# Eight attention heads on five engines: count products set among the scores, the last bias added early, a send moved by six blocks

## What is computed

```python
def gat_layer(x, W, a_src, a_dst, bias, src, dst, heads, out_c, concat):
    h = (x @ W).reshape(n, heads, out_c)
    al_s = jnp.einsum('nhc,hc->nh', h, a_src)
    al_d = jnp.einsum('nhc,hc->nh', h, a_dst)
    e = jax.nn.leaky_relu(al_s[src] + al_d[dst], NEG_SLOPE)
    m = jax.ops.segment_max(e, dst, num_segments=n)
    ex = jnp.exp(e - m[dst])
    z = jax.ops.segment_sum(ex, dst, num_segments=n)
    out = jax.ops.segment_sum(h[src] * (ex / (z[dst] + 1e-16))[:, :, None], dst, num_segments=n)
    out = out.reshape(n, heads * out_c) if concat else out.mean(axis=1)
    return out + bias
# block 3
h = gat_layer(x, W1, a_src1, a_dst1, b1, src, dst, heads=8, out_c=96, concat=True)
h = jax.nn.elu(h)
out = gat_layer(h, W2, a_src2, a_dst2, b2, src, dst, heads=1, out_c=768, concat=False)
x = _layernorm(x + out)
```

## Time and profile before

| | |
|---|---|
| median of three runs | 1436.75 us (1436.01 to 1437.41) |
| profiled execution, its own time | 1437.73 us |
| its span, first to last instruction | 1436.0 us, mean granted clock 0.991 |
| TensorE busy | 1367.7 us (95%) |
| VectorE, ScalarE, GpSimd busy | 762.8, 441.9, 559.0 us |
| chain of work that ended last | PE 76%, DVE 13%, ACT 4%, issue 3%, POOL 3%, DMA 1% |
| the one-head layer of block 2, its score steps | about 1115 to 1143 us |
| the eight heads | about 1266 to 1352 us |
| the last layer | about 1352 to 1436 us |

### The profile page before, as it was taken

The page is one execution under the profiler, slowest core; times in us unless marked ns, Lnnn a source line. Parts: engine busy times, 40 slices in busy tenths (PEclk is TensorE's granted clock), DMA queues, the critical chain, the costliest instruction groups (busy, mean ns, idle before and its releaser), DMA issues.

```text
span 1436.0 us, 22503 instructions
## 1 busy us (share of the span) xinstructions
PE 1367.7 (95%) x7784; PEld 1274.6 (89%) x7784; DVE 762.8 (53%) x1818; ACT 441.9 (31%) x936; POOL 559.0 (39%) x629
## 2 busy tenths in 40 slices
PE   5999999999999999999999999999998999988997
PEld 3676999999999999999999999999888887878874
DVE  6876755224544356474232434765375504599644
ACT  1564521102010000100110222255574424467631
POOL 8000324324243525343442423143433463548830
PEclk9999999999999999999999999999999999998999
DMA  3101111113333223242211211221101310200001
GB/s 117 55 29 34 39 34 50 50 34 109 105 107 105 67 89 115 72 131 68 67 55 45 68 53 46 61 83 57 56 23 39 107 53 17 82 18 1 1 11 54
DMA packets 57804, 86.49 MB, mean 60 GB/s; under 512 B 6468, under 2 KB 54459, under 8 KB 57584
## 3 DMA queue, kind: packets, MB, share of 16 engines
q1 hardware_dynamic: 45204, 65.82, 15.8%
q10 hardware_dynamic: 12504, 19.36, 4.4%
HBM read 83.24 MB, written 1.92 MB: 59 GB/s over the span
## 4 chain that ended last, share of the span: by engine, by line
PE 76%; DVE 13%; ACT 4%; issue 3%; POOL 3%; DMA 1%; DVEq 0%; SPq 0%; ACTq 0%; POOLq 0%
PE psum L2487 13%; PE psum L2491 13%; PE psum L2490 13%; PE psum L2504 7%; PE psum L2507 7%; PE psum L2988 4%; DVE max_scratch L2189 3%; PE psum L2636 3%; PE psum L2561 2%; POOL w_lo L919 2%; PE psum L2530 1%; PE psum L2533 1%; PE psum L2476 1%; DVE more_tiles L2233 1%; DVE score_tiles L2233 1%
## 5 line engine op out<-in xcount | busy, mean ns | idle before, releaser
L2487 PE MATMUL psum<-w_lo,xT_hi 128*125 128x384 f32 (+4 forms) x1110 | 377.4, 340 | 3.3 <-POOL w_lo L919 1.8
L2491 PE MATMUL psum<-w_hi,xT_hi 128*125 128x384 f32 (+4 forms) x1110 | 373.4, 336 | 0.0
L2490 PE MATMUL psum<-w_hi,xT_lo 128*125 128x384 f32 (+4 forms) x1110 | 373.3, 336 | 0.0
L906 POOL CAST w_hi<-w_raw 128x384 fp32r<-128x384 f32 x190 | 105.2, 553 | 569.7 <-PE psum L2491 466.0
L1093 ACT ACTIVATE h_hi<-psum 125x384 fp32r<-125x384 f32 (+1 forms) x120 | 59.1, 492 | 529.3 <-PE psum L2491 524.9
L1739 DVE TENSOR_TENSOR h_lo<-psum,h_hi 125x384 fp32r<-125x384 f32 (+1 forms) x120 | 66.9, 558 | 288.0 <-ACT h_hi L1093 287.2
L2487 PEld LDWEIGHTS psum<-w_lo,xT_hi 128*125 128x125 f32 (+1 forms) x1110 | 205.9, 186 | 6.1 <-POOL w_lo L919 3.4
L908 POOL TENSOR_TENSOR w_lo<-w_raw,w_hi 128x384 fp32r<-128x384 f32 x190 | 201.2, 1059 | 15.2
L2490 PEld LDWEIGHTS psum<-w_hi,xT_lo 128*125 128x125 f32 (+1 forms) x1110 | 206.4, 186 | 0.4
L2491 PEld LDWEIGHTS psum<-w_hi,xT_hi 128*125 128x125 f32 (+1 forms) x1110 | 206.0, 186 | 0.0
L2504 PE MATMUL psum<-h_lo,adjacency 125*125 125x384 f32 (+3 forms) x600 | 203.5, 339 | 2.1 <-issue 1.9
(11 more groups left out here) (350 smaller groups left out, 2272.2 us busy)
## 6 DMA issues: line engine op xcount, KB each, us to landing
w_raw<-weights_dram SPq DMA_DIRECT2D x296, 192.0 KB, 2.4
score_w_raw<-weights_dram ACTq DMA_DIRECT2D x58, 192.0 KB, 2.8
x_nat<-x_dram SPq DMA_DIRECT2D x1, 1875.0 KB
x_residual<-x_dram SPq DMA_DIRECT2D x5, 375.0 KB
score_a_rows<-L_gnn_a_src_dram ACTq DMA_DIRECT2D x8, 192.0 KB, 3.3
score_a_rows<-L_gnn_a_dst_dram ACTq DMA_DIRECT2D x8, 192.0 KB, 4.5
out_dram<-x_residual SPq DMA_DIRECT2D x4, 375.0 KB
rgcn_bias<-rgcn_bias_dram SPq DMA_DIRECT2D x1, 1125.0 KB
```

The source lines that it names most:

```text
L906: nc.gpsimd.tensor_copy(mem.wh[:, slot, :], mem.raw[:, raw_slot, :]).then_inc(w_hi_ready, 1)
L2487: ins = nc.tensor.matmul(o, h, wl, start=(j == 0), stop=False, skip_group_check=True)
L2490: nc.tensor.matmul(o, l, wh, start=False, stop=False, skip_group_check=True)
L2491: ins = nc.tensor.matmul(o, h, wh, start=False, stop=stop and j == k - 1, skip_group_check=True)
```

## The change

Four edits:

1. `Q1` sends its columns at block 22 instead of 16 (`LONG_EVENTS`); `Q3` keeps 16.
2. VectorE's two `finish` of a head move from the next round into the head's own scores, behind score 2, and `columns` moves from before score 4 to before score 2.
3. ScalarE takes the exponent of tile 2 before the below-zero step of tile 3, and GpSimd's round becomes: product of tile 2 of h+1, `unit_sum(h-1)`, products of tiles 3 and 4, `unit_bias(h)`.
4. The bias of `Q3` is loaded into `par[0]` ahead of `Q2`'s features, with a semaphore of its own, and GpSimd's five adds stand ahead of the first head's products.

```diff
+LONG_EVENTS = {3: (("scores", 0),), 6: (("row", 0),), 22: (("send", 0),)}
...
-Q1 = Attention(Q0, 1, D, K8, PIECES, True, BASE_L2B, True, PAIR_EVENTS, {})
+Q1 = Attention(Q0, 1, D, K8, PIECES, True, BASE_L2B, True, LONG_EVENTS, {})
...
-        LATE = 3
+        LATE, COLUMNS_AT, FINISH_AT = 3, 2, 2
...
+            pool.wait_ge(last_bias_loaded, 16)
+            pool.wait_ge(xT_lo_ready, T_Q[2] + UNITS)
+            for m in range(NB):
+                r = mem.xres[0:BP, m, :]
+                nc.gpsimd.tensor_tensor(r, r, mem.par[0][0:BP, 0:D], ALU.add).then_inc(res_biased, 1)
+
+            def late_products(h, a, e):
 
-            def late_products(h):
-
-                for i, counts in enumerate(late_counts):
+                for i, counts in list(enumerate(late_counts))[a:e]:
...
-            late_products(0)
+            late_products(0, 0, LATE)
             for h in range(LAST):
-                late_products(h + 1)
-                unit_bias(h)
+                late_products(h + 1, 0, 1)
                 if h:
                     unit_sum(h - 1)
+                late_products(h + 1, 1, LATE)
+                unit_bias(h)
             unit_sum(LAST - 1)
             split_to(NCHUNKS)
-
-            pool.wait_ge(params_loaded, 16 * 9)
-            pool.wait_ge(cols_ready, Q3.head0 + 1)
-            for m in range(NB):
-                r = mem.xres[0:BP, m, :]
-                nc.gpsimd.tensor_tensor(r, r, mem.par[1][0:BP, 0:D], ALU.add).then_inc(res_biased, 1)
...
             load_row("L3_gnn_b1", par[1], D)
+            load_part("L3_gnn_b2", par[0], 0, D, last_bias_loaded)
...
                 source_below(h, NB - LATE)
-                for k in range(NB - LATE, NB):
+                source_exp_below(h, NB - LATE)
+                source_below(h, NB - LATE + 1)
+                for k in range(NB - LATE + 1, NB):
                     if k + 1 < NB:
                         source_below(h, k + 1)
                     source_exp_below(h, k)
...
-            load_row("L3_gnn_b2", par[1], D)
...
                 for k in range(NB):
-                    if k == NB - 1 and h + 2 < HEADS3:
+                    if k == COLUMNS_AT and h + 2 < HEADS3:
                         columns(Q2, h + 2)
                     score(Q2, h, k)
+                    if k == FINISH_AT:
+                        for i in range(NB - LATE):
+                            finish(Q2, h, i)
...
                 if h:
                     head_z(h - 1)
-                for k in range(NB - LATE):
-                    finish(Q2, h, k)
                 if h + 3 < HEADS3:
                     maxima(Q2, h + 3)
```

More of the change, by code:

```diff
@@ L565, in program @@
         b2_loaded = sem("b2_loaded")
+        last_bias_loaded = sem("last_bias_loaded")
         pre_loaded = [sem(f"pre_loaded{i}") for i in range(PRE_RING)]
```

## The result

The changed kernel takes 1456.4 us (1456.07 to 1458.61, four runs), the kernel before 1436.67 beside it: 1.014 times as long, interval 1.0123 to 1.0158. That is 19.7 us slower; forecast were 14.5, 1451.2, with a range to 1456.0. The profiled execution has a span of 1454.9 for 1436.0, 18.9 more.

What follows compares the result with a forecast made beforehand. TensorE is busy nearly throughout; in the heads VectorE sets turns 1 to 4, ScalarE 5 and 6. Heads +16.8, send +1.4, last layer -3.7 give +14.5 on the median 1436.75: 1451.2 us, range 1439 to 1456.

Steps and rivals of the forecast that it cites:

- The bound before: Eight heads, kernel before: VectorE sets turns 1 to 4 at 11.4 us, ScalarE turns 5 and 6 at 9.4.
- Turn 0: First score of head 0 to that of head 1: +3.6 us, columns waiting for two bias adds; lower bound +1.5.
- Turns 1 and 2: Heads 1 and 2, GpSimd not yet behind: turns of 10.4 and 11.0 us, free of its contention.
- Turn 6: Head 6, no columns left: 10.4 + 2.0 = 12.4 us against 9.4, +3.0.
- Turns 3 to 5: Heads 3 to 5, GpSimd behind: 11.0 plus 1.8 us contention (bounds 0 and 2.9), turns of 12.8.
- The end: Head 7's first score to the end of TensorE's sum: 17.2 us for 11.87, +5.3, waiting for GpSimd's products.
- The send: One-head layer: TensorE stops 1.58 us earlier but resumes 1.4 later, +1.4; bounds -1.6 and +1.4.
- The last layer: Without GpSimd's five adds: -1.9 us from freed count products, -1.8 from TensorE's higher clock; -3.7, bounds -1.9 and -3.7.
- the clock term: Last layer's first sum: with its wait down to 1.5 us, TensorE runs at 2.4 GHz, -1.8.
- Rival (a): Heads: GpSimd's wait doesn't collide, columns and products run alone; +2.9 us, 1439.7; chance 0.12.
- Rival (b): Heads: VectorE alone sets turns 1 to 4 at 10.4, last two turns stay 9.4; faster, 1427.5 us; chance 0.09.
- Rival (c): Heads: columns wait three times, TensorE falls to 1.2 GHz in longer gaps before its sums; +20 or so, 1457; chance 0.07.

Runs made afterwards that it cites:

- the products back in the next round: The changed kernel with VectorE's two count products of a head moved back from among its scores into the next round: 1448.83 us, 1.0087 times the kernel before.
- the pair free: The kernel before with GpSimd's first product of a head waiting for VectorE's two count products of that head: 1436.81 us, 0.9995 times.
- without the heads' orders: The kernel before with only the last bias loaded ahead of the heads and GpSimd's five adds ahead of the first head's products: 1436.61 us, 0.9993 times.
- the heads alone: The kernel before with only the new orders of VectorE, ScalarE and GpSimd in the eight heads; send and bias as before: 1455.45 us, 1.0126 times.
- the last round put back: The changed kernel, but in the last round GpSimd makes all three products of head 7 before unit_sum of head 5: 1452.7 us, 1.011 times.
- the send alone: The kernel before with only the one-head layer's send moved to block 22 from 16: 1439.44 us, 1.0014 times.
- GpSimd's order back: The changed kernel with GpSimd's round as before (three products, bias add, unit_sum last): 1443.93 us, 1.0046 times the kernel before.
- ScalarE's order back: The changed kernel with ScalarE's below-zero steps of tiles 2 and 3 again before the exponent of tile 2: 1459.15 us, a single execution.

## Why the prediction was right and wrong, point by point

Direction, mechanism and place were right: slower, through the heads, by GpSimd's wait for the elu and ScalarE's loop closing over VectorE's fourth score. The time lies 0.4 beyond the upper end of the range, since two terms of the sum were taken too low: the price of contention in turns 3 to 5, and the clock at the end of the heads. The range itself was drawn narrow: with the prediction's own upper bound for the heads, +22, the sum is 1456.5.

- **The bound before** (VectorE in turns 1 to 4, ScalarE in 5 and 6): right. With the products back in the next round turn 6 is 9.5, and with the pair free turns 1 and 2 are 10.3, for the 10.4 that the step gives VectorE without contention.
- **Turn 0, +3.6**: right, 13.6; the two shares, ScalarE's wait and the adds, show apart in the kernels without the adds (11.6) and without the heads' orders (12.8). They overlap: 1.6 and 2.8 apart, 3.6 together.
- **Turns 1 and 2, 10.4 and 11.0**: right (10.7, 10.9). **Turn 6, 12.4**: right in number, but its "2.0" for the pair of products has no row; the price that the prediction had read for the pair was 1.0. The pair waits for two GpSimd instructions there and costs 2.1 more than alone, so the hit is in part luck.
- **Turns 3 to 5, "I take 1.8 for a turn in which GpSimd is behind, bounds 0 and 2.9"**: the mis-sized term, and the step that failed. It measured 13.5 - 11.0 = 2.5. The step was right that columns and products don't both pay here, but then took a middle value for which it had no row; three columns at the price that it had read, 0.95 for 0.16, are already 2.4. The columns stand first, and three of them together take 3.2 for 0.5, since they wait for instructions of 1.20 to 1.51 and not of one microsecond as in the earlier trace rows. So they take the whole stretch and the products none. That is 0.7 more in each of three turns, 2.1 together.
- **The end, "the last ten to twenty matmuls (0.115 each) at 17.2"**: 18.7, 1.5 more. GpSimd's products came nearly as computed, 16.0 for 15.7; the last 20 matmuls ran at 0.2 each, mostly at the lower clock. In the kernel with the heads alone, without that clock, the end is 17.4. The ten matmuls behind them cost 1.4 that no step had. In the kernel with the last round put back TensorE keeps the upper level and both go.
- **The send, +1.4**: right by the means over all profiles, 1.4, and within what the kernel with the send alone measured (0.7 to 3.3), though the two profiles side by side show 0.45.
- **The last layer, -3.7**: -2.0 and -1.6, right. How much the clock term gives depends on the execution of the kernel before that it is measured against: 0 to 3.0 by the profiles with the long wait (last section), so its size is in part luck.

So of the 4.4 between forecast (14.5) and spans (18.9), 2.1 is the columns, 1.5 the end (1.2 by the clock, 0.3 by later products), 1.4 the ten slow matmuls, 0.3 small terms, and -0.95 the send, whose load happened to land sooner in this pair; the rest to 19.7 is the difference of spans and medians.

The Trainium skill (SBUF — State Buffer, "Who interferes with whom") calls contention for the ports which VectorE and GpSimd share an exclusive lock; that one engine has them for a whole instruction and the other is fully blocked it states for VectorE's two-port modes, in which VectorE uses the shared ports beside its own. Here the trace shows the like for VectorE's instructions with two SBUF inputs: in turn 3 each waiting column ends 0.02 to 0.03 after a GpSimd instruction does. So an instruction of 5 elements a partition waited as long as one of 625 (up to 1.3 and 1.15 us), and the tiny columns could cost more, 2.7, than the two products in the same place, 2.2. The page also has it that a VectorE instruction with two SBUF inputs contends with a GpSimd instruction that reads SBUF; there the measurement differs for one kind, as the next section but one tells.

Rival (a), no collision, falls: columns waited in each late turn. Rival (b), faster, falls: even with GpSimd's order, send and bias as before, the interleaving costs 5.8. Rival (c), columns waiting three times and TensorE at 1.2 GHz in longer gaps, given 0.07 and +20 or so, came closest: in turns 3 to 5 three columns wait, and TensorE's clock falls in the gap ahead of the last sum, and costs time there and just behind.

## What to carry to other kernels

Where two engines lock each other out by whole instructions, ask which instruction stands first in the other's busy stretch, and count instructions, not elements: here a chain of tiny ones paid 2.7 and two full tiles 2.2. An instruction that one engine makes only at the end of its turn should not be waited for in the middle of another engine's queue; behind that queue's other work of the round it cost 13.6 us less here. Work that collides is best put into a stretch where its engine idles and the other uses one input: that alone made this kernel 4.1 us faster, while moving it ahead of the heads gave nothing that can be told from noise.

## What the runs showed of the hardware

- GpSimd's two-input TENSOR_TENSOR held VectorE's columns, its TENSOR_SCALAR did not: with GpSimd's order back, a column at 1315.91 took 0.16 inside a TENSOR_SCALAR that reads SBUF and runs from 1314.93 for 1.81, and the same in turns 3 and 5.
- The lock works both ways: beside VectorE's pair GpSimd's bias add took 1.77 and a product 1.85, for 1.20 and 1.29 in turn 3.
- The same instructions after the same waits got different clocks in different executions. At the start of the eight-head layer's features TensorE waits 0.86 and 1.29 in all; in 6 of the 14 kernels' profiles, among them that of the kernel with the heads alone, ten matmuls that follow take 0.54 for 0.34 each and the heads start some 1.6 later. Five of the six have the send at block 22, of seven such kernels; the seventh, with ScalarE's order back, has its slow matmuls 14 us earlier. Of the seven kernels with the send at 16 only the one with the heads alone has them. So the moved send may bring on the low clock and cost more than its 1.4; one profile of each kernel doesn't show it. In the kernel with the heads alone, one of the ten, and the stretch with its PEclk of 0.50:

```profile
1242.41 0.54 PE L2492 MATMUL psum<-w_lo,xT_hi 128*125 128x400 f32 x1
```

```profile
1242.00:1245.00 3.00, 3.00 (x10) 2.94 (x10) 0.00 (x0) 0.64 (x2) 1.00 (x1) 0.50 0.26 94
```

- So too the last layer's first sum: after a wait of 3.42 it took 8.29 before, 9.68 with GpSimd waiting for the pair, 8.39 in two others, and 6.70 in the kernel with VectorE's and ScalarE's orders alone:

```profile
1398.58 6.70 PE L3014 MATMUL psum<-features,score_tiles 125*125 125x385 f32 x20 [3.43 <-DVE score_tiles L2244]
```

After 1.42 or 1.43 it took 6.70 in all nine kernels with that wait. What decides in the longer wait stays open; a clock term read from one execution has that spread.
- A parameter load of the same size took 10.25 to 11.38 from issue to landing in the 14 profiles, 11.38 being the kernel before, so a microsecond on a chain through it can come and go between two profiles.
